# Rotation products of the latent stage: sines on GpSimd, cosines ahead of the inverse roots

## The chip, the cores and the metric

One core of a Trainium2 chip runs the whole program in one launch. The metric is the device time of that core in microseconds (us). Its engines are TensorE (PE, with its weight loads as PEld), VectorE (DVE), ScalarE (ACT), GpSimd (POOL) and SyncE (SP, which issues DMAs).

## What is computed

A tower of two layers over 4096 tokens (32 tiles of 128 tokens) with 192 features, all in float32: an embedding with attention, a routed attention stage, a latent attention stage, and a last block of attention with a mixture of experts. The change is in the latent stage. Of it, this much matters here (12 heads of 16 elements, `latent` being a compressed form of the token):

```python
q, k, v = split(latent @ w_qkv)            # per head of 16 elements
q = rope(rmsnorm(q, qn_w)); k = rope(rmsnorm(k, kn_w))
# rope(x) = x * cos + concat(-x2, x1) * sin, x1 and x2 the halves (8 + 8) of a head
q_f, k_f = elu(q) + 1, elu(k) + 1          # features
...
x = x + attention(q_f, k_f, v) @ w_proj * silu(latent @ w_outgate)
xn = rmsnorm(x, ffn_ln_w)
x = x + silu(xn @ w1) * (xn @ w2) @ w3
```

The root mean square of a head does not depend on the rotation, so the kernel rotates the raw product (a table of cosines and one of sines hold the weights `qn_w`, `kn_w` too) and multiplies by the inverse root behind it.

## The kernel before

The latent stage works on two streams (`streams`, stream 0 and stream 1, with buffers of their own in the regions `WK` and `R`) of M = 2 tiles each, NG = 8 times over: 16 pairs of tiles. The work on one pair is two generators for each engine, a first part (`vector_l_1`, `tensor_l_1`, `scalar_l_1`, `pool_l_1`) that ends with the attention's output, and a second part (`..._l_2`) with the projection and the feed-forward block. `in_turns_apart` writes the first part of one stream in turns with the second part of the other, from `yield` to `yield`, and so fixes the order on each engine by hand. I call one such stretch a half: there are 17, the first with a first part alone, 15 with both, and the last with a second part alone. Each engine works strictly in its own order and waits on semaphores (`f.cat`, `f.root` and so on; `ch.step` is VectorE waiting for its own instruction).

In a half with both parts, the places of the change and of the steps around it are these.

- ACT takes the products of `latent` with the q and k weights out of PSUM, once squared into `a.a` (L1671) and once plain into `a.qk` (L1672), one tile at a time, and counts `f.cat`.
- DVE sums the squares of tile 0 (L1454, L1455), then does the scaling of the other stream's rows for the feed-forward block (L1535, two instructions, of the second part; they wait for `f.root` of POOL), then sums tile 1 (L1454, L1455). Nine small instructions make the inverse root of 48 numbers a row (`inverse_roots`, L1412 to L1420).
- DVE then makes the four products with the sines (L1464, L1465, for q and for k, 192 elements a row each, in runs of 8) into `a.b`, the two products with the cosines (L1468, 384 elements a row each) into `a.a`, the difference for the gates (L1471), their sum (L1472), and for each tile the multiplication by the inverse root (L1475) and the minimum with zero (L1477). The last frees the exponential on ACT (L1688), which needs a table load in front of it.
- DVE puts the features together (L1484) and counts `f.pads`. On that PE turns them (L1617, 12 transposes). In front of L1617 in PE's order stand the turning of the other stream's rows (L985, L987), which waits for L1535, and its 32 products with the feed-forward weights (L1591, L1594), which wait for ACT's L993.
- ACT (L1692) and DVE (L1492) take the turned features out of PSUM, between them come the SiLU of the other stream (L1719 on ACT, with a table load) and its gating (L1541 on DVE), then PE multiplies q by k (L1565) and DVE applies the decay (L1507).
- POOL has only the roots in this stage (`roots`, L1047): one of 4 numbers and two of 2 numbers a row in a half.

```python
            inverse_roots(ch, a.rs[:, 0:24 * M], a.ve[:, 0:24 * M], a.nt)
            v4 = [x.rearrange("p (t s h d) -> p t s h d", t=M, s=2, d=DH) for x in (a.qk, a.a, a.b)]
...
        def pool_l_1(pool, g, a, f):
            roots(pool, a, f, per(g, 3, 1), 2 * M)
            yield
```

Two other lines outside this stage are used for their durations: L523, in which POOL adds a bias to 384 elements a row while DVE quantises (L414, 768 elements a row), and L2394, a POOL product of 4 elements a row beside DVE's L221 (768 elements a row, two inputs in SBUF).

Of the kernel before, what the change touches and what calls it, by code (L numbers as in the profile page):

```python
# [10 lines left out]
ALU = mybir.AluOpType  # L11
# [5 lines left out]
P = 128  # L17
# [3 lines left out]
H = 12  # L21
DH = 16
# [13 lines left out]
def per(g, n, k):  # L36

    return g * n + k
# [57 lines left out]
def tower(nc, a, out):  # L96

    with ExitStack() as ctx:
# [3 lines left out]
        def sem(name):  # L102
            return ctx.enter_context(nc.semaphore(name))
# [651 lines left out]
        class Region:  # L755
# [5 lines left out]
            def take(self, n):  # L761
                self.at += n
                assert self.at <= self.x.shape[1], self.at
                return self.x[:, self.at - n:self.at]

        def chunks2(x):
            return x.rearrange("p (c n) -> p c n", c=2)
# [116 lines left out]
        M = 2  # L884
# [61 lines left out]

        for n, a in enumerate(streams):
            a.n, a.bank = n, bank[4 * n:4 * n + 4]
            a.sems = [sem(f"pair{n}_{i}") for i in range(34)]
            a.hs, a.x, a.xr, a.sq = take(M * D, M), take(M * D, M), take(M * D, M), take(M * D, M)  # L950
            a.xT = chunks2(take(2 * NM))
            a.st, a.mv, a.ve, a.rs = take(6 * M, M), take(2 * M, M), take(24 * M), take(24 * M)
# [6 lines left out]
        def tiles_of(g, a):  # L959
            return tiles(resid[:, bass.ds((g * 2 + a.n) * (M * D), M * D)])  # L960
# [394 lines left out]
        l_cw, l_sw = take(2 * DH, 2), take(2 * DH, 2)  # L1355
# [4 lines left out]
        def l_signals(a):  # L1360

            s = Own()
            s.var, s.root, s.x, s.squared, s.xr, s.xT_p, s.xT, s.lat_p, s.lat, s.cat_p, s.cat, s.gates, s.gate_in, \
                s.gate_t, s.features_in, s.features_exp, s.value, s.pads, s.slots_p, s.slots, s.qk_p, s.decayed, \
                s.oT_p, s.oT, s.out_p, s.out, s.proj_p, s.ffn_in, s.hid_p, s.silu, s.hid, s.ffn_p, \
                s.gate_s, s.slots_v = a.sems[0:34]
            return s

        def heads(x):
            return x.rearrange("p (h d) -> p h d", d=DH)  # L1370
# [38 lines left out]
        def inverse_roots(ch, y, x, t):  # L1409

            yi = y.bitcast(I32)
            ch.step(nc.vector.tensor_scalar(yi, x.bitcast(I32), 1, None, ALU.arith_shift_right))  # L1412
            ch.step(nc.vector.tensor_scalar(yi, yi, -1, 0x5f3759df, ALU.mult, ALU.add))
            ch.step(nc.vector.tensor_tensor(t, y, y, ALU.mult))
            ch.step(nc.vector.tensor_tensor(t, t, x, ALU.mult))
            ch.step(nc.vector.scalar_tensor_tensor(out=y, in0=t, scalar=-3.0, in1=y, op0=ALU.add, op1=ALU.mult))
            ch.step(nc.vector.tensor_tensor(t, y, y, ALU.mult))
            ch.step(nc.vector.scalar_tensor_tensor(out=t, in0=t, scalar=0.25, in1=x, op0=ALU.mult, op1=ALU.mult))
            ch.step(nc.vector.scalar_tensor_tensor(out=t, in0=t, scalar=-10.0 / 3.0, in1=t, op0=ALU.add, op1=ALU.mult))
            ch.step(nc.vector.scalar_tensor_tensor(out=y, in0=t, scalar=5.0, in1=y, op0=ALU.add, op1=ALU.mult))  # L1420

        def norm_stats(v, ch, g, a, f, eps):

            for i in range(M):
                ins = nc.vector.bn_stats(a.st[:, i, :], tiles_of(g, a)[:, i, :])
            ch.step(ins)
            for i in range(M):
                ins = nc.vector.bn_aggr(a.mv[:, i, :], a.st[:, i, :])
            ch.step(ins)
            ch.step(nc.vector.tensor_scalar(a.ve[:, 0:M], a.mv[:, :, 1], 1e-5, None, ALU.add))  # L1430
            nc.vector.scalar_tensor_tensor(out=a.ve[:, M:2 * M], in0=a.ve[:, 0:M], scalar=eps, in1=a.mv[:, :, 1],  # L1431
                                           op0=ALU.mult, op1=ALU.add).then_inc(f.var, 1)
# [12 lines left out]
        def vector_l_1(v, ch, g, a, f):  # L1445

            norm_stats(v, ch, g, a, f, 1e-6)
            yield
            v.wait_ge(f.root, per(g, 3, 1))
            yield from twice_normed(v, ch, g, a, f, f.xr)  # L1450
            for i in range(M):
                v.wait_ge(f.cat, per(g, M, i + 1))
                ve = a.ve[:, 24 * i:24 * i + 24]
                ch.step(nc.vector.tensor_reduce(ve, heads(a.a[:, 384 * i:384 * i + 384]), X, ALU.add))  # L1454
                ins = nc.vector.tensor_scalar(ve, ve, 1.0 / DH, 1e-6, ALU.mult, ALU.add)  # L1455
                if i == 0:
                    yield
            ch.step(ins)
            inverse_roots(ch, a.rs[:, 0:24 * M], a.ve[:, 0:24 * M], a.nt)
            v4 = [x.rearrange("p (t s h d) -> p t s h d", t=M, s=2, d=DH) for x in (a.qk, a.a, a.b)]  # L1460
            for s in range(2):
                q4, a4, b4 = [x[:, :, s] for x in v4]
                bc = lambda w: w.unsqueeze(1).unsqueeze(1).to_broadcast([P, M, H, w.shape[1]])
                nc.vector.tensor_tensor(b4[:, :, :, 0:8], q4[:, :, :, 8:16], bc(l_sw[:, s, 0:8]), ALU.mult)  # L1464
                ins = nc.vector.tensor_tensor(b4[:, :, :, 8:16], q4[:, :, :, 0:8], bc(l_sw[:, s, 8:16]), ALU.mult)  # L1465
            for s in range(2):
                q4, a4, b4 = [x[:, :, s] for x in v4]
                ins = nc.vector.tensor_tensor(a4, q4, bc(l_cw[:, s, :]), ALU.mult)  # L1468
            ch.step(ins)
            v.wait_ge(f.gates, per(g, 1, 1))  # L1470
            nc.vector.tensor_tensor(a.z, a.sg[:, :, :, 1], a.sg[:, :, :, 3], ALU.subtract).then_inc(f.gate_in, 1)  # L1471
            ch.step(nc.vector.tensor_tensor(a.qk, a.a, a.b, ALU.add))  # L1472
            for i in range(M):
                w = slice(384 * i, 384 * i + 384)
                ch.step(nc.vector.tensor_tensor(heads(a.a[:, w]), heads(a.qk[:, w]),  # L1475
                                                a.rs[:, 24 * i:24 * i + 24].unsqueeze(2).to_broadcast([P, 24, DH]), ALU.mult))
                nc.vector.tensor_scalar(a.b[:, w], a.a[:, w], 0.0, None, ALU.min).then_inc(f.features_in, 1)  # L1477
            ch.step(nc.vector.tensor_scalar(a.pz, a.sg[:, :, :, 2], 1.0, None, ALU.add))
            ch.step(nc.vector.scalar_tensor_tensor(out=a.amp, in0=a.sg[:, :, :, 0], scalar=1.0, in1=a.pz, op0=ALU.add,
                                                   op1=ALU.mult))  # L1480
            for i in range(M):
                v.wait_ge(f.features_exp, per(g, M, i + 1))
                w = slice(384 * i, 384 * i + 384)
                nc.vector.scalar_tensor_tensor(out=a.pad[:, i, :, 0:DH], in0=heads(a.a[:, w]), scalar=0.0,  # L1484
                                               in1=heads(a.qk[:, w]), op0=ALU.max, op1=ALU.add).then_inc(f.pads, 1)
            v.wait_ge(f.gate_t, per(g, 2, 1))
            ch.step(nc.vector.tensor_scalar(a.pz, a.z2, -2.0, 1.0, ALU.mult, ALU.add))
            nc.vector.scalar_tensor_tensor(out=a.pz, in0=a.pz, scalar=l_temp, in1=a.amp, op0=ALU.mult,
                                           op1=ALU.mult).then_inc(f.gate_in, 1)
            for i in range(M):  # L1490
                v.wait_ge(f.slots_p, per(g, M, i + 1))
                nc.vector.tensor_copy(a.ts[:, i, 3:6, :], a.bank[2 * i + 1][:, 0:384].rearrange("p (k n) -> p k n", k=3)  # L1492
                                      ).then_inc(f.slots_v, 1)
            yield
            decayed(v, g, a, f, 0)
            v.wait_ge(f.gate_t, per(g, 2, 2))
            ch.step(nc.vector.tensor_scalar(a.z, a.z, 0.6, 0.5, ALU.mult, ALU.add))
            ch.step(nc.vector.tensor_scalar(a.z, a.z, 0.05, 0.95, ALU.max, ALU.min))
            nc.vector.tensor_tensor(a.va[:, :, :, 0:DH], a.r.rearrange("p t (h d) -> p t h d", d=DH),
                                    a.z.unsqueeze(3).to_broadcast([P, M, H, DH]), ALU.mult).then_inc(f.value, 1)  # L1500
            decayed(v, g, a, f, 1)
# [45 lines left out]
        def pool_l_1(pool, g, a, f):  # L1547
            roots(pool, a, f, per(g, 3, 1), 2 * M)
            yield

        def pool_l_2(pool, g, a, f):
            roots(pool, a, f, per(g, 3, 2))
# [886 lines left out]
```

## Time and profile before

| | us |
|---|---|
| median of 3 runs | 2158.04 |
| lowest and highest | 2157.45, 2159.05 |
| the profiled execution's own time | 2150.94 |
| its span | 2149.0 |
| busy: PE, PEld | 1588.4 (74%), 1159.9 (54%) |
| busy: DVE, ACT, POOL | 1313.1 (61%), 976.7 (45%), 392.7 (18%) |

The span is the time from the first to the last instruction that the profiler recorded. The engines' busy times overlap. All times of single instructions below are microseconds from the start of that span, and durations marked "ns" are nanoseconds. The latent stage runs from about 745 to 1245 us.

### The profile page before, as it was taken

The page shows a single profiled execution, that of the slowest core. Times are in us where ns is not written, and L with a number is a line of the kernel's source. Part 1 is how long each engine was busy: PE and PEld are TensorE (multiplying, and loading weights), DVE is VectorE, ACT ScalarE, POOL GpSimd, SP SyncE. Part 2 cuts the span into 40 slices and gives each one's busy share as a digit, 9 for nine tenths or more (in the row PEclk, how much of TensorE's full clock was granted, in tenths as well). Part 3 has the DMA queues.
Part 4 walks back from the last instruction along what each step waited for, and adds up shares of the span by engine and source line. Part 5 has one row for each costly group of instructions (what it writes and reads, how often), then busy time and mean ns, then how long its engine had stood idle before and what let it go on. Part 6 is the DMA issues. An engine that isn't in the chain of part 4 may idle for free.

```text
span 2149.0 us, 35471 instructions
## 1 busy us (share of the span) xinstructions
PE 1588.4 (74%) x12058; PEld 1159.9 (54%) x12058; DVE 1313.1 (61%) x4372; ACT 976.7 (45%) x2770; POOL 392.7 (18%) x480
## 2 busy tenths in 40 slices
PE   0166665967776358888888858888888849999996
PEld 0032224855555235555555536666666637777774
DVE  7899885877777567888788725555555532212221
ACT  1367998833333344555545413333333314344442
POOL 7302331000000000000000001221222213333332
PEclk9975555577787669999999967777777859999998
DMA  3000001099900000000000000000000036777775
GB/s 71 13 1 1 1 1 20 3 173 194 164 0 0 1 1 1 0 0 0 0 0 0 1 0 12 23 18 17 20 22 22 23 105 169 177 185 177 177 177 133
DMA packets 136260, 112.98 MB, mean 53 GB/s; under 512 B 29416, under 2 KB 128456, under 8 KB 136136
## 3 DMA queue, kind: packets, MB, share of 16 engines
q1 hardware_dynamic: 119320, 91.70, 18.0%
q0 software_dynamic: 16864, 20.33, 5.0%
q8 instruction: 40, 0.66, 0.1%
q14 instruction: 36, 0.29, 0.1%
HBM read 69.19 MB, written 45.94 MB: 54 GB/s over the span
## 4 chain that ended last, share of the span: by engine, by line
PE 53%; DVE 26%; ACT 13%; issue 5%; POOL 1%; DVEq 1%; SPq 0%; DMA 0%; another core or an unknown queue 0%; ACTq 0%; POOLq 0%
ACT bank L716 8%; PE bank L2255 7%; PE bank L1007 7%; PE bank L2240 5%; PE bank L2244 3%; PE bank L1926 3%; PE bank L966 3%; PE bank L1000 2%; PE bank L1591 2%; PE bank L1184 2%; PE bank L1939 2%; DVE WK L1778 1%; DVE WK L1507 1%; DVE R L1507 1%; DVE R L1778 1%
## 5 line engine op out<-in xcount | busy, mean ns | idle before, releaser
L1047 POOL TENSOR_TENSOR WK<-WK,mhalf 128x2 f32<-128x2 f32 (+1 forms) x96 | 77.9, 812 | 919.1 <-DVE WK L1431 344.7
L2292 ACT ACTIVATE R<-bank,WK 128x256 f32<-128x256 f32 x234 | 98.3, 471 | 217.5 <-PE bank L2244 217.5
L2147 DVE SCALAR_TENSOR_TENSOR WK<-bank,R,WK 128x192 f32<-128x192 f32 x78 | 29.0, 414 | 267.5 <-PE bank L2255 267.5
L1007 PE MATMUL bank<-WK,R 96*128 96x256 f32 x576 | 174.7, 459 | 15.9 <-ACT WK L973 11.0
L716 ACT ACTIVATE bank<-bank,nbias,sc 128x128 f32<-128x128 f32 x384 | 168.9, 954 | 22.6 <-POOL nbias L528 22.6
L2176 POOL DMA_INDIRECT moe_sum<-WK x78 | 121.7, 1560 | 263.9 <-DVE WK L2147 197.0
L2255 PE MATMUL bank<-R 128*128 128x192 f32 x936 | 169.1, 331 | 0.0
L716 ACT ACTIVATION_READ_ACCUMULATOR bank<-bank,nbias,sc 128x1 f32 x384 | 162.1, 728 | 0.0
L2255 PEld LDWEIGHTS bank<-R 128*128 128x128 f32 x936 | 150.1, 190 | 13.3 <-issue 13.3
L1007 PEld LDWEIGHTS bank<-WK,R 96*128 96x128 f32 x576 | 128.8, 233 | 43.4 <-ACT WK L973 16.5
L966 PE MATMUL bank<-ident,WK 128*96 128x128 f32 x320 | 68.1, 351 | 96.6 <-DVE WK L1030 69.2
L2240 PE MATMUL bank<-R 128*128 128x256 f32 x468 | 126.2, 392 | 1.1 <-ACT R L2283 1.1
L1926 PE MATMUL bank<-WK 32*128 32x128 f32 x1536 | 83.6, 365 | 33.8 <-DVE WK L1778 13.0
L610 PE MATMUL bank<-R 32*128 32x128 bf16 x384 | 62.8, 300 | 60.0 <-ACT bank L716 57.2
L966 PEld LDWEIGHTS bank<-ident,WK 128*96 128x96 f32 x320 | 43.4, 157 | 113.6 <-DVE WK L1030 69.3
L2240 PEld LDWEIGHTS bank<-R 128*128 128x128 f32 x468 | 84.5, 192 | 21.1 <-issue 13.3
L1926 PEld LDWEIGHTS bank<-WK 32*128 32x128 f32 x1536 | 68.6, 253 | 48.9 <-DVE WK L1778 15.2
L610 PEld LDWEIGHTS bank<-R 32*128 32x128 bf16 x384 | 29.5, 118 | 118.8 <-ACT bank L716 106.7
L433 DVE TENSOR_REDUCE neg_all<-bank 128x3 f32<-128x384 f32 x128 | 69.5, 554 | 27.3 <-PE bank L610 25.2
L1591 PE MATMUL bank<-WK,R 128*128 128x256 f32 x256 | 73.6, 410 | 15.0 <-ACT WK L993 15.0
L973 ACT ACTIVATE WK<-bank 96x512 f32<-96x512 f32 x48 | 28.5, 593 | 123.3 <-PE bank L966 123.3
L2244 PE MATMUL bank<-R 64*128 64x256 f32 x468 | 82.8, 431 | 0.0
(492 smaller groups left out, 3913.9 us busy)
## 6 DMA issues: line engine op xcount, KB each, us to landing
moe_rows_in<-zeros SPq DMA_DIRECT2D x1, 25026.0 KB, 139.3
R<-in_L_ffn_w SPq DMA_DIRECT2D x39, 576.0 KB
R<-in_L_ffn_w SPq DMA_DIRECT2D x39, 384.0 KB
R<-moe_rows_in SPq DMA_DIRECT2D x39, 194.0 KB, 4.6
R<-in_L_ffn_w SPq DMA_DIRECT2D x78, 96.0 KB
WK<-in_L_ffn_b SPq DMA_DIRECT2D x39, 96.0 KB
moe_sum<-resid POOLq DMA_DIRECT2D x16, 192.0 KB
moe_sum<-WK POOLq DMA_INDIRECT x78, 6.0
```

The costliest lines, as they stand in the source:

```text
L610: mm = nc.tensor.matmul(bank[u % 4][:, k * P:(k + 1) * P], qk[32 * j:32 * j + 32, k, i * P:(i + 1) * P], qk[32 * j:32 * j + 32, 3 + k, i * ...
L716: ins = nc.scalar.activation(s, s, ACT.Exp, bias=nbias[:, u, k:k + 1], scale=col(SS), accum_out=units(sum_all, g, u)[:, k:k + 1])
L966: mm = nc.tensor.transpose(a.bank[b][0:C, c * NM + i * P:c * NM + (i + 1) * P], src[:, i, c * C:(c + 1) * C], ident[:, :])
L1007: mm = nc.tensor.matmul(out, w[0:C, c, m], a.xT[0:C, c, :], start=(c == 0), stop=(c == 1))
L1047: nc.gpsimd.tensor_tensor(a.rs[:, 0:n], a.ve[:, 0:n], mhalf[:, 0:n], ALU.pow).then_inc(f.root, 1)
L1591: nc.tensor.matmul(a.bank[c][:, out], wa[:, c * P:(c + 1) * P], a.xT[:, 0, :], start=True, stop=False)
L1926: mm = nc.tensor.matmul(a.bank[j][:, k * P:(k + 1) * P], x, y, start=True, stop=True)
L2176: pool.indirect_dma_start(out=acc, out_offset=bass.IndirectOffsetOnAxis(ap=x_id[k % B3][:, t:t + 1].bitcast(U32), axis=0), in_=x_y[k % B3] ...
L2240: nc.tensor.matmul(bank[b + n][:, 0:NR], xw_1a[h][:, q * P:(q + 1) * P], x_T[h][:, 0, :], start=True, stop=False)
L2244: mm = nc.tensor.matmul(bank[b + n][:, 0:NR], xw_1b[h][s, p * P:(p + 1) * P], x_T[h][s, 1, :], start=False, stop=True)
L2255: mm = nc.tensor.matmul(bank[4 + t][:, 0:D], x_hid[f][:, t * P:(t + 1) * P], xw_2[h][:, f, :], start=(p == 0 and n == 0), stop=(p == PAIRS ...
L2292: ins = nc.scalar.activation(x_hid[q], bank[(0, 2, 0)[p] + n][:, 0:NR], ACT.Gelu, bias=xb_1[h][:, q:q + 1])
```

## The change

The four products with the sines leave VectorE for GpSimd: they are written into `pool_l_1`, behind a wait for both tiles of `f.cat`, and count a new semaphore `f.rotated` (number 34 of each stream's list). VectorE makes the two products with the cosines in front of `inverse_roots` and waits for `f.rotated` in front of the sum of both.

```diff
@@ -946,7 +946,7 @@
-            a.sems = [sem(f"pair{n}_{i}") for i in range(34)]
+            a.sems = [sem(f"pair{n}_{i}") for i in range(35)]
@@ -1363,7 +1363,7 @@
-                s.gate_s, s.slots_v = a.sems[0:34]
+                s.gate_s, s.slots_v, s.rotated = a.sems[0:35]
@@ -1419,6 +1419,9 @@
+        def over_heads(w):
+            return w.unsqueeze(1).unsqueeze(1).to_broadcast([P, M, H, w.shape[1]])
+
@@ -1456,19 +1459,14 @@
             ch.step(ins)
+            for s in range(2):
+                q4, a4 = [x.rearrange("p (t s h d) -> p t s h d", t=M, s=2, d=DH)[:, :, s] for x in (a.qk, a.a)]
+                ins = nc.vector.tensor_tensor(a4, q4, over_heads(l_cw[:, s, :]), ALU.mult)
+            ch.step(ins)
             inverse_roots(ch, a.rs[:, 0:24 * M], a.ve[:, 0:24 * M], a.nt)
-            v4 = [x.rearrange("p (t s h d) -> p t s h d", t=M, s=2, d=DH) for x in (a.qk, a.a, a.b)]
-            for s in range(2):
-                q4, a4, b4 = [x[:, :, s] for x in v4]
-                bc = lambda w: w.unsqueeze(1).unsqueeze(1).to_broadcast([P, M, H, w.shape[1]])
-                nc.vector.tensor_tensor(b4[:, :, :, 0:8], q4[:, :, :, 8:16], bc(l_sw[:, s, 0:8]), ALU.mult)
-                ins = nc.vector.tensor_tensor(b4[:, :, :, 8:16], q4[:, :, :, 0:8], bc(l_sw[:, s, 8:16]), ALU.mult)
-            for s in range(2):
-                q4, a4, b4 = [x[:, :, s] for x in v4]
-                ins = nc.vector.tensor_tensor(a4, q4, bc(l_cw[:, s, :]), ALU.mult)
-            ch.step(ins)
             v.wait_ge(f.gates, per(g, 1, 1))
             nc.vector.tensor_tensor(a.z, a.sg[:, :, :, 1], a.sg[:, :, :, 3], ALU.subtract).then_inc(f.gate_in, 1)
+            v.wait_ge(f.rotated, per(g, 1, 1))
             ch.step(nc.vector.tensor_tensor(a.qk, a.a, a.b, ALU.add))
@@ -1547,6 +1545,12 @@
         def pool_l_1(pool, g, a, f):
             roots(pool, a, f, per(g, 3, 1), 2 * M)
             yield
+            pool.wait_ge(f.cat, per(g, M, M))
+            for s in range(2):
+                q4, b4 = [x.rearrange("p (t s h d) -> p t s h d", t=M, s=2, d=DH)[:, :, s] for x in (a.qk, a.b)]
+                nc.gpsimd.tensor_tensor(b4[:, :, :, 0:8], q4[:, :, :, 8:16], over_heads(l_sw[:, s, 0:8]), ALU.mult)
+                ins = nc.gpsimd.tensor_tensor(b4[:, :, :, 8:16], q4[:, :, :, 0:8], over_heads(l_sw[:, s, 8:16]), ALU.mult)
+            ins.then_inc(f.rotated, 1)
```

On DVE, in the loop's half with the first part of stream 1, behind the sums of the squares, this stood before (`c_v` is VectorE's wait for itself, `pair1_11` is `f.gates`):

```order
L1419 TENSOR_TENSOR WK<-WK 128x48 [waits c_v]
L1420 SCALAR_TENSOR_TENSOR WK<-WK 128x48 [waits c_v]
L1464 TENSOR_TENSOR R<-R 128x2x12x8 [waits c_v]
L1465 TENSOR_TENSOR R<-R 128x2x12x8
L1464 TENSOR_TENSOR R<-R 128x2x12x8
L1465 TENSOR_TENSOR R<-R 128x2x12x8
L1468 TENSOR_TENSOR R<-R 128x2x192 x2
L1471 TENSOR_TENSOR R<-WK 128x24 [waits pair1_11,c_v]
L1472 TENSOR_TENSOR R<-R 128x768
```

The same place of the changed kernel, from the other stream's scaling on (L1533 is L1535 of before, L1457 and L1458 are L1454 and L1455, L1464 is now the product with the cosines; `pair1_10` is `f.cat`, `pair0_1` is `f.root` of stream 0):

```order
L1533 TENSOR_SCALAR WK<-WK 128x192 [waits pair0_1]
L1533 TENSOR_SCALAR WK<-WK 128x192
L1457 TENSOR_REDUCE WK<-R 128x24 [waits pair1_10]
L1458 TENSOR_SCALAR WK<-WK 128x24 [waits c_v]
L1464 TENSOR_TENSOR R<-R 128x2x192 [waits c_v]
L1464 TENSOR_TENSOR R<-R 128x2x192
L1412 TENSOR_SCALAR WK<-WK 128x48 [waits c_v]
L1413 TENSOR_SCALAR WK<-WK 128x48 [waits c_v]
```

The cosines now stand between the sums and the inverse roots, the sines are gone from DVE, and what was L1472 (L1470 of the changed kernel) waits for `pair1_34`, which is `f.rotated`.

On POOL, the changed kernel has this in the loop (`pair1_0` and `pair0_0` are the `f.var` of the two streams; L1548 is the wait for `f.cat`'s value); before, only the rows of L1047 stood there:

```order
L1047 TENSOR_TENSOR WK<-WK,mhalf 128x4 [waits pair1_0]
L1047 TENSOR_TENSOR WK<-WK,mhalf 128x2 [waits pair0_0] x2
L1551 TENSOR_TENSOR R<-R 128x2x12x8 [waits pair1_10]
L1552 TENSOR_TENSOR R<-R 128x2x12x8
L1551 TENSOR_TENSOR R<-R 128x2x12x8
L1552 TENSOR_TENSOR R<-R 128x2x12x8
L1047 TENSOR_TENSOR WK<-WK,mhalf 128x2 [waits pair1_0] x2
```

The four products stand behind all three roots of the half and ahead of those of the next half.

## Rows read from the trace of the kernel before

**Rows 1.** Busy time by stretch of the latent stage; count, clock share, DMA share, GB/s
```profile
945.00:1000.00 55.00, 45.87 (x389) 31.35 (x388) 44.84 (x141) 29.05 (x74) 4.54 (x6) 0.97 0.00 0
1115.00:1170.00 55.00, 45.73 (x372) 30.58 (x374) 44.41 (x135) 28.94 (x74) 3.91 (x5) 1.00 0.00 0
```

**Rows 2.** Chain that ended last, one half: start, us, what
```profile
979.58 0.36 DVE R L1464
...
980.75 0.95 DVE R L1468 x2
...
985.21 1.28 ACT L1719
986.51 0.66 ACT R L1719 x2
987.16 0.77 ACT R L1692 x2
```

**Rows 3.** Timeline of PE, same half: start, us, instruction, [idle before <-releaser]
```profile
976.79 0.33 PE L985 MATMUL bank<-ident,WK 128*128 128x128 f32 x1 [0.21 <-DVE WK L1535]
...
985.20 0.70 PE L1594 MATMUL bank<-WK,R 64*128 64x256 f32 x4
985.83 1.53 PE L1617 MATMUL bank<-ident,R 128*128 128x128 f32 x12
988.10 0.95 PE L1565 MATMUL bank<-R 32*128 32x128 f32 x24 [0.74 <-DVE R L1492]
```

**Rows 4.** Timeline of DVE, same half
```profile
976.18 0.55 DVE L1535 TENSOR_SCALAR WK<-WK 128x192 f32<-128x192 f32 x2
976.65 0.55 DVE L1454 TENSOR_REDUCE WK<-R 128x24 f32<-128x384 f32 x1
977.23 0.18 DVE L1455 TENSOR_SCALAR WK<-WK 128x24 f32<-128x24 f32 x1
...
979.58 0.36 DVE L1464 TENSOR_TENSOR R<-R 128x192 f32<-128x192 f32 x1
...
980.66 1.02 DVE L1468 TENSOR_TENSOR R<-R 128x384 f32<-128x384 f32 x2
981.72 0.20 DVE L1471 TENSOR_TENSOR R<-WK 128x24 f32<-128x24 f32 x1
981.84 0.95 DVE L1472 TENSOR_TENSOR R<-R 128x768 f32<-128x768 f32 x1
...
986.74 1.21 DVE L1492 COPY R<-bank 128x384 f32<-128x384 f32 x2 [0.35 <-PE bank L1617]
```

**Rows 5.** Timeline of ACT, same half
```profile
975.65 0.51 ACT L1672 ACTIVATE R<-bank 128x384 f32<-128x384 f32 x1
...
987.05 0.88 ACT L1692 ACTIVATE R<-bank 128x384 f32<-128x384 f32 x2
```

**Rows 6.** Timeline of POOL, same half
```profile
974.76 0.76 POOL L1047 TENSOR_TENSOR WK<-WK,mhalf 128x2 f32<-128x2 f32 x1 [5.41 <-DVE WK L1043]
996.16 1.01 POOL L1047 TENSOR_TENSOR WK<-WK,mhalf 128x4 f32<-128x4 f32 x1 [20.64 <-DVE WK L1431]
```

**Rows 7.** PE in the first half; and who waited, whole stage (us, times, longest)
```profile
773.06 2.15 PE L1617 MATMUL bank<-ident,WK 128*128 128x128 f32 x9 [8.05 <-DVE WK L1484]
...
PE bank L1617 <- DVE WK L1484: 8.1, 1, 8.1
```

**Rows 8.** Single lines: count, ns min/median/max, first and last start
```profile
L523 POOL TENSOR_TENSOR resid<-resid,bprojb x16: 991/992/994, 181.8 to 340.2; 128x384 f32<-128x384 f32 x16
L2394 POOL TENSOR_TENSOR shift<-less_mean,rs x8: 193/446/740, 30.0 to 88.8; 128x4 f32<-128x4 f32 x8
L414 DVE TENSOR_SCALAR WK<-WK,sc x8: 620/1207/1210, 163.3 to 298.2; 128x768 f32<-128x768 f32 x8
L1535 DVE TENSOR_SCALAR WK<-WK x32: 312/315/321, 797.3 to 1238.0; 128x192 f32<-128x192 f32 x32
L1464 DVE TENSOR_TENSOR R<-R x16: 350/355/359, 800.7 to 1212.2; 128x192 f32<-128x192 f32 x16
```

**Rows 9.** Timelines of DVE and POOL where L414 and L523 meet
```profile
213.65 1.21 DVE L414 TENSOR_SCALAR WK<-WK,sc 128x768 f32<-128x768 f32 x1
...
213.45 0.99 POOL L523 TENSOR_TENSOR resid<-resid,bprojb 128x384 f32<-128x384 f32 x1
```

**Rows 10.** Timelines of DVE and POOL where L221 and L2394 meet
```profile
49.87 0.96 DVE L221 SCALAR_TENSOR_TENSOR WK<-resid,pos 128x768 f32<-128x768 f32 x1
...
50.20 0.69 POOL L2394 TENSOR_TENSOR shift<-less_mean,rs 128x4 f32<-128x4 f32 x1
```

## The prediction

> **What bounds the kernel now.** I first read the busy times by stretch, to see whether one engine is full in the latent stage. None is: in 55 us PE is busy 45.87 us and DVE 44.84 us, POOL 4.54 us [rows 1]. So the stage is held by waits in turns, and POOL looks free. Then I read the chain of waits for one half of the loop (975 to 989 us). It runs through DVE, the products with the sines and cosines included, into ACT's table load and L1719, L1692 [rows 2]. By that alone each microsecond taken from DVE would be won. The timelines of the engines, read side by side, say otherwise. PE starts L1617 at 985.83, in the very moment in which its feed-forward products end (L1594, 985.20 and 0.70 long, its last matmul overlapping), with no idle time in front [rows 3]: the features were not what it waited for. DVE idles 0.35 us for L1617 before L1492, and both copies of L1492 end at 986.74 + 1.21 = 987.95; ACT's L1692 ends at 987.05 + 0.88 = 987.93 [rows 4, 5]. PE's L1565 waits for both and starts at 988.10 [rows 3]. Two chains thus end together: DVE to ACT, and L1535 (DVE) to L985 to the feed-forward products to L1617 (PE). This is the pattern of all 15 halves with both parts. Only in the first half, which has no feed-forward products, did PE idle for the features (8.05 us, once) [rows 7].
>
> **What leaves DVE.** The four products with the sines take DVE from 979.58 to 980.66, start to start: 1.08 us a half [rows 4]. The two with the cosines (1.02 us) only move. If this came through in 16 halves it would be 17.3 us. By the two chains, hardly any does: the second six transposes of L1617 end at 985.83 + 1.53 = 987.36, and the second L1692 starts at about 987.43, so ACT coming earlier gains at most 0.07 us, of which L1492 (to 987.95) leaves 0.02. I take 0 for the 15 halves, and up to 1.08 us for the first.
>
> **What POOL takes.** No row shows this form on POOL. The nearest: 384 elements a row take 992 ns, 4 elements 193 ns undisturbed [rows 8]. That is 0.19 us of set-up and 2.1 ns an element, so 0.19 + 192 × 0.0021 = 0.59 us a product, 2.4 us for four. Bounds: 0.19 us each below, 0.99 us each above (the long row, should runs of 8 elements cost double). I take 0.59, since the long row too has two float32 inputs in SBUF, the second one repeated. POOL has nothing else to do: its last root of the half ends at 975.52 and the next begins at 996.16 [rows 6]. It starts when ACT's L1672 ends (975.65 + 0.51 = 976.16) plus some 0.08 us, so at 976.24 [rows 5]. Undisturbed it would be ready at 978.6; DVE wants the result at L1472, now 981.84, then at most 1.08 us sooner, 980.76 [rows 4]. The new wait is covered by 2.1 us, and still by 0.5 us with 0.99 us a product. The DVE queue behind that wait is therefore not held.
>
> **What POOL's work does to DVE.** Here lies the price. DVE's L414 takes 620 ns alone and 1207 ns beside POOL's L523 [rows 8]. In the rows of one meeting POOL works from 213.45 to 214.44 and L414 from 213.65 to 214.86: DVE did its 0.40 us of data (768 elements, two at a time) only after POOL had ended [rows 9]. The other way round, POOL's product of 4 elements took 0.69 us instead of 0.19 when DVE's L221, with two inputs in SBUF, had begun before it: POOL ended at 50.89, just behind DVE at 50.83 [rows 10]. So the two engines exclude each other in such pairs. L1535 is of the first kind: 315 ns for 192 elements, less than the 355 ns of the two-input L1464 on as many [rows 8], so it too moves two at a time. The cosines and L1414 to L1420 are of the second. That POOL stops a two-input instruction of DVE no row shows; between 0 and 0.59 us for each product, I take what L414 lost in kind: the part of the product in which data move, 0.40 us.
>
> The Trainium skill, page "SBUF — State Buffer", section "Who interferes with whom", says the same more strongly: a VectorE instruction with two SBUF inputs contends with a GpSimd one that reads SBUF, and whichever issues first keeps the shared ports for its whole instruction. By that rule the loss would be up to 0.59 us a product, which is the second rival below. The trace agrees in the two directions that it shows (1207 for 620 ns, 0.69 for 0.19 us).
>
> Now in order. The first product starts at 976.24, and its data begin at about 976.43. L1535 starts at 976.18 and 976.41 [rows 4]; the data of its second instruction would start at about 976.6. I take it that POOL is first. Then L1535 ends at about 977.02 instead of 976.73: **d = 0.29 us**, between 0 and 0.59. L985 and the whole PE chain behind it, through L1617, start later by d. The data of the second product lie under the reduction L1454, which has one input. The third and the fourth come between L1455, the cosines and the first small instructions: 2 × 0.40 = 0.80 us. DVE's balance at L1472: −1.08 + 0.29 + 0.80 = **0.0 us**. The DVE and ACT chain keeps its time, the PE chain loses d, and each half ends when the later one does.
>
> **The sum.** 15 × 0.29 = 4.4 us slower; the first half, without L1535, has a balance of about 0 too. The new semaphore and its clearing are some instructions of tens of nanoseconds, three times in all: nothing. Against the profiled execution's 2150.94 us this is 2155.3. The median of the runs is 7.1 us above that execution, and the same 4.4 us on it give 2158.04 + 4.4 = 2162.4 us. A measurement of this kernel tells about 0.2% (4.3 us) from no change, so the forecast lies right on that edge.
>
> **The rivals.**
>
> *POOL comes second, and nothing changes.* Place: the second L1535. If the first product's data start more than about 0.17 us later than I think (976.6 instead of 976.43), L1535 is through and d = 0. The rest falls on DVE, whose balance is 0, and the PE chain covers any gain. 2158 us, with 1 us less from the first half. For it: L1535 is issued 0.06 us before POOL starts, and its pair is back to back. Against it: 0.17 us is long beside POOL's set-up of 0.19. It is not slower.
>
> *Whole instructions exclude each other, or DVE never gets in between.* Then L1535 loses 0.3 us, the end of the second product 0.2 us beyond the reduction, the third and fourth 0.59 us each: −1.08 + 1.67 = +0.59 us on the DVE and ACT chain, which has some 0.04 us of slack. 15 × 0.55 = 8.3 us: 2166 us. This is the case that the page's rule above would give.
>
> *Short runs are slow on POOL.* At 0.99 us a product the data part is 0.80 us; d = 0.7, the second product reaches 0.4 us past the reduction, two more take 0.8 each: −1.08 + 2.7 = +1.6 us, 15 times 24 us: 2182 us.
>
> *The chain of waits is right.* DVE is what every half waits for, the products vanish from it, POOL disturbs nothing: 16 × 1.08 = 17.3 us: 2140.8 us. For it speaks only the chain [rows 2], which follows one of two chains that end within 0.02 us.
>
> **How the numbers follow.** Chances: forecast 0.35, POOL second 0.28, whole instructions 0.24, short runs of 8 elements 0.08, the chain's 17 us 0.05. Predicted time 2162.4 us. The range takes in the forecast, POOL second with its microsecond, and the whole-instruction case up to some 0.95 us a half: 2156.5 to 2172.5. It leaves out short runs of 8 elements and the 17 us, and something at the edges. Forecast alone would lie between 2160 and 2165. Faster by over 0.2%: 0.05 and 0.02 for a sum of small gains, 0.07. Within: 0.26 of POOL second and somewhat over a third of the forecast, 0.39. Slower: 0.54.
>
> **What would show it.** In the changed profile: POOL's four products at 0.6 us or, where DVE holds them up, 0.8 to 1.0 us; L1535 (now L1533) with a median well over 315 ns for its second instruction, and PE's L985 later behind `f.cat` by as much; one of the two cosine products well over 555 ns; hardly any wait of DVE for the new semaphore; PE still without idle time in front of the turning of the features. The period of two halves would be 0.6 us longer. I am wrong if L1533 stays at 315 ns (then POOL second), if that period grows by over 1 us (whole instructions), or if it shrinks, which means that PE was not the cover.

## The result and the profile after

| | us |
|---|---|
| before, 9 runs | 2159.05 median (2157.45 to 2163.88) |
| changed kernel, 9 runs | 2165.5 median (2164.22 to 2167.5) |
| ratio | 1.0028, 95% interval 1.0018 to 1.0038 |
| changed kernel, profiled execution | 2166.38, span 2164.4 |

The change makes the kernel slower by 0.28% by the ratio, 6.0 us on 2159.05; the two medians lie 6.45 us apart. The forecast was 4.4 us. Most of the loss comes about as forecast. Two terms were off: one was 0.33 us a half instead of 0.29, and the TensorE clock, which the sum left out, took 1.4 us in the two profiled executions.

The two profiled executions lie 15.4 us apart in their spans, more than the runs do. From the start to the first end of L1676 (L1672 of before) they differ by 2.1 us, in the latent stage from there to the last first-of-a-half L1676 by 5.8 us (450.59 for 444.78), and by 7.5 us in what follows, which holds the sines of the last of the 16 first parts and then only work that the change does not touch. Executions scatter there whatever the kernel: two of the kernel before, on one and the same other chip, ended 923.2 and 928.6 us after that last mark. So below only times inside the latent stage are compared.

The chain of waits of the changed kernel, over the same half as [rows 2] (start, us, what; the first rows are 2.1 us later here, those from L985 on 2.5 us):

```profile
977.04 0.49 ACT R L1676
...
977.63 0.56 DVE WK L1457
...
978.32 0.89 DVE WK L1533 x2
...
979.25 0.33 PE bank L985
...
981.51 1.13 PE bank L1595 x4
...
987.73 0.63 PE bank L1598 x4
988.36 1.47 PE bank L1621 x12
```

Before, this view ran through the sines, the cosines and ACT's table load. Now it runs through the other chain, L1533 and PE's feed-forward products. Of two chains that ended together, the second now ends last.

DVE in that half (compare [rows 4]):

```profile
978.21 0.18 DVE L1458 TENSOR_SCALAR WK<-WK 128x24 f32<-128x24 f32 x1
978.32 0.88 DVE L1533 TENSOR_SCALAR WK<-WK 128x192 f32<-128x192 f32 x2
979.12 0.54 DVE L1457 TENSOR_REDUCE WK<-R 128x24 f32<-128x384 f32 x1
979.69 0.53 DVE L1458 TENSOR_SCALAR WK<-WK 128x24 f32<-128x24 f32 x1
980.25 1.36 DVE L1464 TENSOR_TENSOR R<-R 128x384 f32<-128x384 f32 x2
...
983.79 0.20 DVE L1468 TENSOR_TENSOR R<-WK 128x24 f32<-128x24 f32 x1
983.91 0.95 DVE L1470 TENSOR_TENSOR R<-R 128x768 f32<-128x768 f32 x1
...
989.20 1.21 DVE L1490 COPY R<-bank 128x384 f32<-128x384 f32 x2 [0.74 <-PE bank L1621]
```

POOL in that half:

```profile
978.37 0.71 POOL L1551 TENSOR_TENSOR R<-R 128x192 f32<-128x192 f32 x1 [0.93 <-ACT R L1676]
979.04 0.60 POOL L1552 TENSOR_TENSOR R<-R 128x192 f32<-128x192 f32 x1
979.60 0.58 POOL L1551 TENSOR_TENSOR R<-R 128x192 f32<-128x192 f32 x1
980.14 0.59 POOL L1552 TENSOR_TENSOR R<-R 128x192 f32<-128x192 f32 x1
```

PE in that half (compare [rows 3]):

```profile
979.25 0.33 PE L985 MATMUL bank<-ident,WK 128*128 128x128 f32 x1 [0.54 <-DVE WK L1533]
...
987.65 0.70 PE L1598 MATMUL bank<-WK,R 64*128 64x256 f32 x4
988.29 1.53 PE L1621 MATMUL bank<-ident,R 128*128 128x128 f32 x12
990.56 0.95 PE L1569 MATMUL bank<-R 32*128 32x128 f32 x24 [0.74 <-DVE R L1490]
```

To be seen: the pair L1533 takes 0.88 us where it took 0.55, and L985 starts that much later behind it. L1470 follows L1468 without idle time: the new wait holds nothing, since POOL is done at 980.14 + 0.59 = 980.73. PE goes from L1598 to L1621 without a gap, and DVE's idle time in front of the copies L1490 has grown from 0.35 to 0.74 us, because L1621 is later and DVE is not. The single lines (count, ns min/median/max, first and last start; compare [rows 8]) show what a blocked instruction and a free one take (a line with R alone is of stream 1, so of half the first parts):

```profile
L1533 DVE TENSOR_SCALAR WK<-WK x32: 311/320/644, 799.3 to 1246.5; 128x192 f32<-128x192 f32 x32
L1458 DVE TENSOR_SCALAR WK<-WK x32: 177/179/534, 765.5 to 1217.6; 128x24 f32<-128x24 f32 x32
L1464 DVE TENSOR_TENSOR R<-R x16: 544/718/894, 801.2 to 1218.9; 128x384 f32<-128x384 f32 x16
L1551 POOL TENSOR_TENSOR R<-R x16: 579/636/709, 799.3 to 1217.5; 128x192 f32<-128x192 f32 x16
```

**The measure used below.** From the end of a half's first L1672 (L1676) to the next such end is one period. A half with the first part of stream 1 took 28.55 us before and 28.87 now, the others 29.79 and 30.12, at full clock. The same is to be read in the rows of POOL's root of four numbers, which comes once a half. Before, every second one is 58.33 us after the last:

```profile
1083.65 1.01 POOL L1047 TENSOR_TENSOR WK<-WK,mhalf 128x4 f32<-128x4 f32 x1 [21.12 <-DVE WK L1431]
...
1141.98 1.01 POOL L1047 TENSOR_TENSOR WK<-WK,mhalf 128x4 f32<-128x4 f32 x1 [21.12 <-DVE WK L1431]
```

In the changed kernel, 58.99:

```profile
1118.19 1.01 POOL L1047 TENSOR_TENSOR WK<-WK,mhalf 128x4 f32<-128x4 f32 x1 [17.88 <-DVE WK L1434]
...
1177.18 1.01 POOL L1047 TENSOR_TENSOR WK<-WK,mhalf 128x4 f32<-128x4 f32 x1 [17.89 <-DVE WK L1434]
```

### The profile page after: what moved, and what is told of

Same layout as the page of the kernel before. It is cut to its first block, busy times and chain, and to the rows that moved or that the text cites. A ratio compares the mean times of both kernels' runs of the same rounds, so it can differ in the third digit from the quotient of the medians.

```text
span 2164.4 us, 35489 instructions
## 1 busy us (share of the span) xinstructions
PE 1597.3 (74%) x12058; PEld 1164.7 (54%) x12058; DVE 1312.9 (61%) x4308; ACT 978.3 (45%) x2770; POOL 432.1 (20%) x544
## 4 chain that ended last, share of the span: by engine, by line
PE 56%; DVE 25%; ACT 12%; issue 4%; POOL 1%; DVEq 1%; DMA 0%; SPq 0%; another core or an unknown queue 0%; ACTq 0%; POOLq 0%
ACT bank L716 8%; PE bank L2259 7%; PE bank L1007 7%; PE bank L2244 5%; PE bank L2248 3%; PE bank L1595 3%; PE bank L1930 3%; PE bank L966 3%; PE bank L1184 2%; PE bank L1598 2%; PE bank L1000 2%; PE bank L1943 2%; DVE WK L1782 1%; DVE WK L1505 1%; DVE R L1505 1%
## 5 line engine op out<-in xcount | busy, mean ns | idle before, releaser
L1047 POOL TENSOR_TENSOR WK<-WK,mhalf 128x2 f32<-128x2 f32 (+1 forms) x96 | 78.1, 813 | 870.1 <-DVE WK L1024 316.7
L1595 PE MATMUL bank<-WK,R 128*128 128x256 f32 x256 | 78.0, 430 | 15.0 <-ACT WK L993 15.0
```

Source lines behind the costliest of these rows:

```text
L1047: nc.gpsimd.tensor_tensor(a.rs[:, 0:n], a.ve[:, 0:n], mhalf[:, 0:n], ALU.pow).then_inc(f.root, 1)
L1595: nc.tensor.matmul(a.bank[c][:, out], wa[:, c * P:(c + 1) * P], a.xT[:, 0, :], start=True, stop=False)
```

## The experiments

They ran on three more chips. On the second were the changed kernel, POOL coming second, the sines left out and the scaling in front (kernel before: 2139.56 median of 35 runs, 2135.27 to 2148.3). On the third were the new order alone, the eight products and the last pair of runs (kernel before: 2138.49, 29 runs, 2132.25 to 2149.38). On the fourth were single executions. Where nothing else is said there are 12 runs of each. Periods are given at full clock, unless it is said otherwise.

**The changed kernel once more.**

> The changed kernel again, as the partner of the others on this chip. Theory (the first product on GpSimd takes the shared access ahead of the second scaling instruction, 0.33 us in each of 15 halves): 1.0020 to 1.0035 of before, undisturbed halves of 28.87 and 30.12 us against 28.55 and 29.79.

Measured 2145.6 us (12 runs), ratio 1.0023 [1.0013 to 1.0034]; periods 28.87 and 30.10 to 30.13, as expected. The loss holds on another chip.

**POOL made to come second.** On the changed kernel, in `pool_l_1` behind the wait for `f.cat`, a wait for the other stream's scaling:

```diff
             pool.wait_ge(f.cat, per(g, M, M))
+            if a.n == 1:
+                pool.wait_ge(l_signals(streams[0]).ffn_in, per(g, 1, 1))
+            elif not (isinstance(g, int) and g == 0):
+                pool.wait_ge(l_signals(streams[1]).ffn_in, per(g, 1, 0))
```

> GpSimd's sines wait until VectorE's two scaling instructions for the feed-forward block are done. Theory (the loss is the second scaling instruction, held up by 0.33 us at the head of TensorE's chain): that instruction is back at 315 ns, halves are back at 28.55 and 29.79 us, time 0.999 to 1.001 of before, so some 5 us under the changed kernel, although the GpSimd work is all there and starts 0.6 us later. Rival (the loss comes from the whole GpSimd work blocking VectorE, or from the new wait in front of the sum): no gain, since both stay: 1.002 to 1.004 of before, or slower still because the sines end later.

Measured 2146.18 us, ratio 1.0012 [0.9996 to 1.0028]. The mechanism is as expected. The line of the scaling (columns as above):

```profile
L1533 DVE TENSOR_SCALAR WK<-WK x32: 311/314/321, 798.3 to 1249.6; 128x192 f32<-128x192 f32 x32
L1464 DVE TENSOR_TENSOR R<-R x16: 868/915/942, 799.6 to 1223.3; 128x384 f32<-128x384 f32 x16
```

No scaling instruction is held any more, both cosine products are (by 0.27 to 0.39 us each), and the undisturbed periods are 28.54 and 29.79 again, those of before. So the 0.33 us a half are the meeting of POOL's first product with the second L1533, and what the cosines lose costs nothing. The total didn't follow: 5 us under the changed kernel were expected, and 2146.18 is no less than its 2145.6. The profiled execution has five stretches of about 10 us at half clock (granted clock 0.50: 1.2 GHz) between 800 and 1225 us, where before's had one of 10.2 and one of 3.4 us. The next question was whether this wait brings them about.

**The same kernel and the one before, looked at again** (a fourth chip, one execution each; nothing is edited).

> A second profile of the kernel in which GpSimd waits for the scaling. Its first profile had the halves of the kernel before (28.55 and 29.79 us) wherever TensorE's clock was full, but five stretches at half clock of 10.2 us each in the latent stage, and its runs lie in two groups, at 2138 to 2141 and at 2146 to 2149 us. If the clock's stretches make the groups, a profile with a time in the lower group has fewer or shorter ones in the latent stage or behind it; if it has as many, the groups come from elsewhere.

> The kernel before once more, for another profile of it: halves of 28.55 and 29.79 us again, and a look at how the stretches of half clock vary from execution to execution (10.2 and 3.4 us between 800 and 1200 us in the first profile).

> The kernel before for a third profile: the same halves, and the same question of how its stretches of half clock vary from execution to execution.

Measured: 2148.01 us with the wait, 2145.76 and 2139.14 for the kernel before (and 2140.87 in a fourth execution, without a profile). By windows over the whole stage (span, then busy us of PE, PEld, DVE, ACT, POOL, granted clock, DMA), the first look at the kernel before, then the second:

```profile
740.00:1250.00 510.00, 400.65 (x3142) 269.81 (x3142) 384.58 (x1196) 249.57 (x648) 39.26 (x48) 0.90 0.00 0
```

```profile
740.00:1250.00 510.00, 396.14 (x3179) 265.77 (x3180) 385.29 (x1198) 250.04 (x652) 39.27 (x48) 0.93 0.00 0
```

One of the stretches in the first of them:

```profile
1154.00:1164.00 10.00, 9.53 (x23) 6.38 (x23) 4.11 (x13) 6.80 (x14) 1.45 (x2) 0.51 0.00 0
```

The unchanged kernel too falls into either of two clock patterns, with the stage (mark to mark) at 456.71 or 444.6 us; the undisturbed periods are 28.54 and 29.79 in both. The wait on `ffn_in` is not needed for it; both profiles of the kernel with the wait fell into the longer one (456.54 us). Of the 12 times with the wait, five lie between 2138.39 and 2140.64 and seven between 2146.09 and 2148.92; of before's 35, eight lie above 2146. The two levels are the same. The shares differ by more than chance easily gives (a difference like this comes up about once in thirty by chance), so whether the wait makes the longer pattern more frequent is open. The levels weigh on every ratio here: it is the periods that tell what an edit does. What sends an execution into one pattern stays open.

**Sines left out on both engines.**

```diff
-            v.wait_ge(f.rotated, per(g, 1, 1))
-            ch.step(nc.vector.tensor_tensor(a.qk, a.a, a.b, ALU.add))
+            ch.step(nc.vector.tensor_tensor(a.qk, a.a, a.a, ALU.add))
```

and the loop with the four products gone from `pool_l_1`.

> The products with the sines are left out on both engines (the sum adds the cosines' product to itself), so VectorE has 1.08 us less in each half and GpSimd disturbs nothing. Theory (TensorE's feed-forward products cover VectorE's work in this place): the 15 halves stay at 28.55 and 29.79 us, only the first half gains, about 1 us in all: 0.999 to 1.000 of before. Rival (the chain of waits through VectorE is what counts): 16 x 1.08 = 17 us, 0.992 of before.

Measured 2138.19 us, ratio 0.998 [0.9965 to 0.9995], a little under the 0.999 to 1.000 expected; none of its 12 times lies above 2143 us, where eight of before's 35 do. The periods are 28.54 and 29.78, unchanged; only the first half is shorter, 32.72 for 33.80, by the 1.08 us that the products had taken. DVE in a later half, whose first plain copy out of PSUM (L1672 of before) ends 2.0 us later than in [rows 4], and then PE:

```profile
987.10 0.24 DVE L1485 SCALAR_TENSOR_TENSOR R<-R,WK 128x24 f32<-128x24 f32 x1
988.78 1.21 DVE L1489 COPY R<-bank 128x384 f32<-128x384 f32 x2 [1.44 <-PE bank L1614]
```

```profile
987.24 0.70 PE L1591 MATMUL bank<-WK,R 64*128 64x256 f32 x4
987.87 1.53 PE L1614 MATMUL bank<-ident,R 128*128 128x128 f32 x12
```

With the products gone altogether, DVE idles 1.44 us in front of the copies instead of 0.35 [rows 4], and L1614 starts where the feed-forward products let it. (L1485, L1489, L1591 and L1614 are L1488, L1492, L1594 and L1617 of before.) This is the most that taking the sines from DVE can give in this order of the work: 1.08 us in the first half, nothing in the 15 others. The rival by the chain of waits, 17.3 us, is refuted.

**The new order alone, sines still on DVE.** On the kernel before, L1468's loop with a `ch.step` of its own in front of `inverse_roots`.

> One part of the change alone: the products with the cosines ahead of the inverse roots, the sines still on VectorE behind them, GpSimd as before. Theory (the loss comes from GpSimd's first product): nothing changes, halves of 28.55 and 29.79 us, 0.9985 to 1.0015 of before. Rival (the new order on VectorE costs something by itself): 1.002 or more.

Measured 2138.63 us, ratio 0.9994 [0.998 to 1.0009]; periods 28.54 and 29.82, first half 33.91 for 33.80. The order of the cosines costs at most 0.03 us a half, a tenth of what the change costs.

**Eight products on POOL instead of four**, the second four into a spare part of `ts`.

> The changed kernel, with GpSimd making each of the four products a second time into a spare buffer, so eight in a row. Theory: the scaling instruction loses the same 0.33 us; four more products fall on the inverse roots, whose small instructions read two tensors, and block VectorE by about 0.4 us each, 1.6 us, which now ends last: halves of 30.2 to 30.5 and 31.4 to 31.8 us, 1.010 to 1.013 of before. Rival (two-input instructions are not blocked, only the two-at-a-time scaling is): as the changed kernel, 1.0025.

Measured 2158.03 us (4 runs), ratio 1.0094 [1.0068 to 1.0121]. DVE behind the held L1533 and L1458:

```profile
985.34 1.76 DVE L1465 TENSOR_TENSOR R<-R 128x384 f32<-128x384 f32 x2
987.14 0.46 DVE L1413 TENSOR_SCALAR WK<-WK 128x48 int32<-128x48 int32 x1
987.63 0.51 DVE L1414 TENSOR_SCALAR WK<-WK 128x48 int32<-128x48 int32 x1
988.17 0.53 DVE L1415 TENSOR_TENSOR WK<-WK 128x48 f32<-128x48 f32 x1
988.74 0.21 DVE L1416 TENSOR_TENSOR WK<-WK 128x48 f32<-128x48 f32 x1
```

POOL beside it:

```profile
985.79 0.90 POOL L1556 TENSOR_TENSOR R<-R 128x192 f32<-128x192 f32 x1
986.65 0.90 POOL L1557 TENSOR_TENSOR R<-R 128x192 f32<-128x192 f32 x1
987.51 0.59 POOL L1556 TENSOR_TENSOR R<-R 128x192 f32<-128x192 f32 x1
...
```

(L1465 is the cosine product here, L1413 to L1421 the inverse root.) L1413 to L1415, which take 0.19 to 0.21 us alone, take 0.46 to 0.53 beside POOL, and POOL takes 0.90 for 0.59 where DVE had begun: the exclusion goes both ways. The second four products cost DVE 0.40 + 0.27 + 0.32 + 0.32 = 1.3 us more (the cosines at 1.76 against the 1.36 above). Now DVE's chain is the later one: in a half at full clock PE waits for the features in front of their turning (L1626 here, L1617 before).

```profile
901.89 1.53 PE L1626 MATMUL bank<-ident,WK 128*128 128x128 f32 x12 [0.70 <-DVE WK L1483]
```

The periods are 29.61 and 30.94, 0.74 and 0.82 us longer than with four products, and less than the expected 30.2 to 30.5 and 31.4 to 31.8: the extra products cost 1.3 us and not 1.6, and DVE had idle time to give. Four of the longer halves last 31.70 us, but each of these holds 3.4 us at half clock. The four products of the changed kernel stay hidden on DVE only because they cost it no more than the 1.08 us that they saved.

**The scaling put in front of the sums**, in the changed kernel: the `yield` at which the other stream's chain may go on stands ahead of the loop instead of inside it, so that both L1535 precede both reductions.

```diff
+            yield
             for i in range(M):
...
-                if i == 0:
-                    yield
```

> The changed kernel with the two scaling instructions ahead of both sums of squares. Theory (two chains end together, TensorE's begins at the scaling): the scaling ends before GpSimd starts, 315 ns each, TensorE's chain starts 0.2 us earlier than before the change (it then waits for its own previous products), VectorE's chain has the relief of 1.08 us less about 0.8 us of blocking and 0.1 us of later sums: halves 0.1 to 0.2 us shorter than before, time 0.998 to 1.000 of before. Rival (GpSimd's blocking of VectorE decides): no better than the changed kernel, 1.002 or more.

Measured 2142.03 us, ratio 0.9998 [0.9979 to 1.0017]; three times lie between 2127.78 and 2129.99 and nine between 2141.02 and 2146.5. The periods are 28.15 and 29.54 to 29.73, so 0.40 and 0.06 to 0.25 us shorter than before, where 0.1 to 0.2 were expected; the stage took 439.84 us. Once more, beside the same edit with the sines on DVE (the kernel before):

> The scaling-first kernel with the sines on GpSimd again, for a second profile and more runs beside its partners: undisturbed halves of 28.15 and 29.54 us, so some 4.9 us less than before in the latent stage, if TensorE's clock falls as often as before: 0.997 to 0.999; where it falls more often, up to 1.001.

> The kernel before with the two scaling instructions ahead of both sums of squares, and no work moved to GpSimd. Theory (two chains that end within some hundredths of a microsecond): TensorE's chain starts earlier, but VectorE's ends 0.2 to 0.4 us later than before, because its sums start later and nothing relieves it; halves of 28.7 to 28.9 and 29.9 to 30.2 us, 1.000 to 1.003 of before, so the gain of the scaling-first kernel needs the sines on GpSimd. Rival (TensorE's chain alone decides): 28.15 and 29.54 us as with the sines on GpSimd, 0.997 to 0.999.

Measured 2133.68 us for the first, ratio 0.9986 [0.9968 to 1.0004], stage 439.7 us, periods as above; 2137.63 us for the second, 0.9996 [0.9981 to 1.0011], periods 28.19 and 29.95. Every second root of four numbers in the kernel with the sines on POOL:

```profile
964.15 1.01 POOL L1047 TENSOR_TENSOR WK<-WK,mhalf 128x4 f32<-128x4 f32 x1 [18.02 <-DVE WK L1434]
...
1022.03 1.01 POOL L1047 TENSOR_TENSOR WK<-WK,mhalf 128x4 f32<-128x4 f32 x1 [18.23 <-DVE WK L1434]
...
1079.73 1.01 POOL L1047 TENSOR_TENSOR WK<-WK,mhalf 128x4 f32<-128x4 f32 x1 [18.02 <-DVE WK L1434]
```

57.88 and 57.70 us for two halves, against 58.33 before and 58.14 with the sines on DVE. The earlier scaling shortens PE's chain, and then DVE's decides in the longer halves. There PE has idle time in front of the turning of the features, first with the sines on POOL (in four of the six such halves between 880 and 1200 us), then with the sines on DVE (in all six; L1620 and L1616 are L1617 of before, L1481 and L1483 its L1484):

```profile
1127.07 1.53 PE L1620 MATMUL bank<-ident,WK 128*128 128x128 f32 x12 [0.23 <-DVE WK L1481]
```

```profile
1131.84 1.53 PE L1616 MATMUL bank<-ident,WK 128*128 128x128 f32 x12 [0.46 <-DVE WK L1483]
```

With the sines on DVE the 29.79 halves even get longer (29.95), which my expectation of 29.9 to 30.2 had, while the short ones got shorter (28.19), which it hadn't. Only with both edits do both halves gain. What moving the sines to POOL is worth appears here, beside the 0.15 us of the first half: 0.26 to 0.44 us for two halves (58.14 to 57.88 or 57.70). The stage is 4.9 us shorter than in the shorter of the looks at before (444.6), of which 1.1 to 1.5 us are fewer and shorter stretches at half clock, yet by the totals neither version can be told from the kernel before. Of the second set's 12 times with both edits, nine lie between 2130.18 and 2136.41 and three between 2143.11 and 2144.98, again two levels.

## Why the prediction was right, and where it was off

- **What bounds the half**: right. PE covers, and the 1.08 us taken from DVE give nothing in 15 halves; leaving them out altogether gave 1.08 us once.
- **POOL's product, 0.59 us**: right, 0.58 to 0.60 undisturbed. Runs of 8 elements cost nothing extra. That rival is refuted.
- **Who is first at the second L1535**: right. POOL started at 978.37, 0.08 us behind the end of L1676's record (977.78 + 0.51 = 978.29), and stopped it. The rival of POOL second did not happen; the experiment with the wait produced it, and the periods of before came back. My forecast gave the two 0.35 and 0.28: that POOL came in first was close to an even guess, not knowledge.
- **d = 0.29 us**: mis-sized, 0.33. My working let POOL's data begin 0.19 us after its start. They did not: the product took 0.71 instead of 0.59 us, held 0.12 us by the first L1533. On the other side the second L1533 ended 0.12 us behind POOL (979.20 behind 979.08), where my 977.02 had it 0.19 behind 976.83. From the start of the pair to its end that is 0.05 + 0.71 + 0.12 = 0.88 us, where I had 0.06 + 0.59 + 0.19 = 0.84: two errors that partly cancel. The periods grew by 0.32 and 0.33: fifteen times 0.325 is 4.9 us.
- **Third and fourth product, 2 × 0.40 us**: 0.35 and 0.34. The third met L1458 (0.53 for 0.18), the fourth the first cosine product (1.36 for 1.02), and in these halves no instruction of the inverse root was met. DVE lost 0.33 + 0.35 + 0.34 = 1.02 us, where I had 1.09, against 1.08 saved. Balance −0.06 instead of 0.0: right.
- **A two-input DVE instruction is stopped too**: assumed then, now shown by the cosines and by L1415. But the rival "whole instructions exclude each other" is refuted: in no meeting looked at did DVE lose a product's whole 0.59 us. In the changed kernel the losses are 0.26 to 0.39 us. The largest seen anywhere is 0.44 (0.62 for 0.18), with the scaling in front, where both engines started at 1002.12 and DVE ended 0.04 us behind POOL. DVE loses what is left of POOL's instruction and no more. The rule of the Trainium skill, page "SBUF — State Buffer", section "Who interferes with whom" (such pairs contend for the shared ports, and the first keeps them for its instruction), agrees with the meetings seen here: the held engine came free when the other's instruction ended (980.22 behind 980.18 us); what I had hung on it, a loss of 0.59 us each, was my reading of it.
- **The first half**: 33.80 to 33.65, −0.15 us. The sum had "about 0". Here DVE is what the half waits for (8.05 us of PE in [rows 7]), and POOL took back 0.93 of the 1.08 us.
- **The clock**: missing from the sum. Stretches at half clock in 800 to 1225 us numbered one of 10.2 and one of 3.4 us before, five of 3.4 us now, in both profiles of the changed kernel. The fifth lies behind the last mark. The others lengthened the periods by 3.87 and 5.24 us in all (now by 0.49, 1.59, 1.58 and 1.58). One of the five, by windows, and PE in it:

```profile
950.50:953.50 3.00, 3.00 (x9) 1.54 (x8) 2.63 (x10) 1.38 (x5) 0.00 (x0) 0.50 0.00 0
```

```profile
949.78 1.64 PE L1595 MATMUL bank<-WK,R 128*128 128x256 f32 x4 [0.94 <-ACT WK L993]
951.36 1.23 PE L1598 MATMUL bank<-WK,R 64*128 64x256 f32 x4
952.51 1.69 PE L1595 MATMUL bank<-WK,R 128*128 128x256 f32 x4
```

Here four products of L1595 take 1.64 and 1.69 us instead of 1.13, L1598 1.23 instead of 0.70. So −0.15 + 15 × 0.325 + (5.24 − 3.87) = 6.1 us, against 6.0 measured. That the two agree so well is in part luck: the clock's 1.4 us are the difference of one pair of patterns, and outside the stage executions scatter by 5 us. The firm comparison is mark to mark inside the stage, where there are 14 such periods beside the first: −0.15 + 4.55 + 1.37 = 5.8 us, as 450.59 − 444.78 gives. That the longer period caused the other pattern is only argued: both changed together, and the kernel before has patterns further apart than that.

## What to carry to other kernels

Before freeing an engine, look for a second chain that ends with the one shown, and leave the work out once: that bounds the gain (here 1.08 us, not 17.3). Work moved to GpSimd was paid here where it met VectorE. DVE lost 1.02 us a half, and only the 0.33 us at the head of the deciding chain cost time. In such a case put that instruction ahead or let GpSimd wait for it, and look at the other chain next.

## What was not expected of the hardware

- The order decides within a tenth of a microsecond. DVE issued the pair L1533 at 978.32 and POOL its product at 978.37; the first of the pair passed and held POOL by 0.12 us, and POOL then got in between two back-to-back DVE instructions.
- A held instruction lost less than the other's length. It looks as if its own start had run already while it waited: L1458 ended 0.04 us behind POOL's product (980.22 behind 980.18), though it takes 0.18 us alone. L1533 grew by 0.33 us, L1464 by 0.34 and L1458 by 0.35 beside products of 0.58 to 0.71 us. POOL's own grew alike, from 0.59 to 0.90 (+0.31).
- One kernel has two clock patterns that repeat, stage 444.6 and 456.7 us, and the totals of before fall into groups near 2139 and 2147 us (in the two looks, 12.1 us more in the stage and 5.4 us less behind it). That is more than the whole effect measured here, and only the undisturbed periods told what an edit does.
